# Re-laid order of the five engines within a unit of a gated delta-rule attention kernel

## The reference, cut to what matters

```python
mixed = einsum('bsh,ch->bsc', layernorm(x), W_qkv)
mixed = silu(causal_conv4(mixed, conv_w))          # q, k, v from it
q, k  = l2norm(q) * DK ** -0.5, l2norm(k)
beta, g = sigmoid(b), cumsum(-exp(A_log) * softplus(a + dt_bias))   # per chunk
A  = -(k_beta @ k.T * decay) * strict
T  = inv(eye - A)                                   # triangular, per chunk
u, kcd = T @ v_beta, T @ (k_beta * exp(g))
for chunk:                                          # the scan
    attn  = (q_i @ k_i.T) * dec_i
    v_new = u_i - kcd_i @ S
    out_i = (q_i * exp(g_i)) @ S + attn @ v_new
    S     = S * exp(g_last) + (k_i * exp(g_last - g_i)).T @ v_new
y = (rmsnorm(out) * norm_w * silu(z)) @ W_out.T
x = x + layernorm(y)
x = x + layernorm(ffn(layernorm(x)))                # weights of the ffn: lut[index]
```

## Time and profile before

| | us |
|---|---|
| median of 3 runs | 4471.09 (4470.88 to 4472.41) |
| the profiled execution, its own time | 4472.62 |
| its span, first to last instruction | 4470.8 |
| PE busy | 4252.6 (95%) |
| DVE busy | 3483.3 (78%) |
| POOL busy | 3039.3 (68%) |
| ACT busy | 2976.3 (67%) |

### The profile page before, as it was taken

The page is one execution under the profiler, slowest core; times in us unless marked ns, Lnnn a source line. Parts: engine busy times, 40 slices in busy tenths (PEclk is TensorE's granted clock), DMA queues, the critical chain, the costliest instruction groups (busy, mean ns, idle before and its releaser), DMA issues. The chain is left out here.

```text
span 4470.8 us, 92997 instructions
## 1 busy us (share of the span) xinstructions
PE 4252.6 (95%) x30644; PEld 3229.0 (72%) x30644; DVE 3483.3 (78%) x7803; ACT 2976.3 (67%) x6124; POOL 3039.3 (68%) x8989
## 2 busy tenths in 40 slices
PE   4899999999999999999999999999999999998798
PEld 2577777777777777777777777777777777777465
DVE  6678888888888888888888888888888888886554
ACT  3576777767776777667777777677767777675211
POOL 1677777777777777777777777777777777776221
PEclk7899999999999999999999999999999999999899
DMA  4222222222232222232222222232222222221200
GB/s 135 54 69 59 62 61 59 63 66 69 45 79 60 60 59 63 61 77 57 57 71 67 60 55 66 63 77 48 67 70 68 56 59 62 67 58 29 67 15 24
DMA packets 592257, 275.23 MB, mean 62 GB/s; under 512 B 464416, under 2 KB 548896, under 8 KB 582560
## 3 DMA queue, kind: packets, MB, share of 16 engines
q1 hardware_dynamic: 591056, 266.66, 24.3%
q0 software_dynamic: 720, 2.62, 0.3%
HBM read 221.87 MB, written 47.30 MB: 60 GB/s over the span
## 5 line engine op out<-in xcount | busy, mean ns | idle before, releaser
L718 DVE SCALAR_TENSOR_TENSOR CV<-pp,CW,CV 128x1023 f32<-128x1023 f32 (+2 forms) x768 | 979.5, 1275 | 30.2 <-ACT CV L1080 18.9
L343 PE MATMUL pp<-A,W 128*128 128x512 f32 x2048 | 966.8, 600 | 31.4 <-DVE CV L718 19.9
L1377 POOL TENSOR_TENSOR UL<-UL,TM 128x126 f32<-128x126 f32 (+22 forms) x1984 | 739.6, 373 | 155.4
L1374 POOL TENSOR_TENSOR TM<-UL,XL 128x126 f32<-128x126 f32 (+22 forms) x1984 | 705.4, 356 | 153.6 <-issue 19.0
L343 PEld LDWEIGHTS pp<-A,W 128*128 128x128 f32 x2048 | 376.6, 193 | 339.7 <-issue 306.8
L1176 ACT ACTIVATE QE<-qa,TAB 128x128 f32<-128x128 f32 x1024 | 316.9, 361 | 407.9 <-PE qa L472 407.8
L838 DVE SCALAR_TENSOR_TENSOR St<-St,TAB,kv 128x128 f32<-128x128 f32 x1024 | 308.5, 343 | 321.5 <-PE kv L491 313.7
L1187 ACT ACTIVATE VS<-qa,EB 128x128 f32<-128x128 f32 x1024 | 318.0, 363 | 297.1 <-PE qa L482 290.9
L535 PE MATMUL emit<-Wo,NTr 128*128 128x256 f32 x2048 | 494.7, 385 | 1.3 <-ACT NTr L1220 1.3
L514 PE MATMUL emit<-Wz,A 128*128 128x256 f32 x2048 | 491.0, 383 | 3.5 <-DVE A L889 3.5
L1080 ACT ACTIVATE CV<-pp,CW 128x1024 f32<-128x1024 f32 x256 | 284.8, 1113 | 233.3 <-PE pp L343 233.3
(11 more groups left out here) (235 smaller groups left out, 9213.9 us busy)
## 6 DMA issues: line engine op xcount, KB each, us to landing
GB<-gcd SPq DMA_DIRECT2D x64, 1024.0 KB, 5.0
W<-wqkv SPq DMA_DIRECT2D x256, 128.0 KB, 3.8
XL<-xb SPq DMA_DIRECT2D x128, 256.0 KB, 4.0
UL<-c_u SPq DMA_DIRECT2D x64, 256.0 KB, 2.9
xb<-X SPq DMA_DIRECT2D x512, 32.0 KB, 1.7
Wz<-wz SPq DMA_DIRECT2D x64, 256.0 KB, 2.8
ub<-UL SPq DMA_DIRECT2D x128, 128.0 KB, 2.9
N<-ub SPq DMA_DIRECT2D x256, 64.0 KB, 2.3
```

The lines of the kernel that those rows point to most:

```text
L343: ins = t.matmul(bk.pp[:, 512 * h:512 * h + 512], m.W[:, c, k, :], m.xnT[:, w // KH % 2, c, 512 * h:512 * h + 512], start=c == 0, stop=c == 1)
L718: v.scalar_tensor_tensor(m.CV[:, t, d:S], bk.pp[:, 0:S - d], m.CW[:, w % KH, t, 3 - d:4 - d], m.CV[:, t, d:S], ALU.mult, ALU.add).then_inc ...
L1374: gp.tensor_tensor(m.TM[:, 0:a, 0:b], m.UL[:, 0:a, k:k + 1].to_broadcast([128, a, b]), m.XL[:, k, k + 1:32].unsqueeze(1).to_broadcast([128 ...
L1377: gp.tensor_tensor(m.UL[:, 0:a, k + 1:32], m.UL[:, 0:a, k + 1:32], m.TM[:, 0:a, 0:b], ALU.subtract).then_inc(s["sub"], 1)
```

## The change

Nothing is computed in another way. The lists of the five engines for one turn of the loop are written in another order. The instruction counts are the same, except for ACT_TABLE_LOAD, which the compiler places: 379 in the program before, 131 now (four fewer in a turn). The core of the diff:

```diff
 main_sp
         for u in range(NU + 2):
+            ldt(u + 1)
             index(u + 2)
-            ldz(u + 1)
-            ldt(u + 1)
             decoded(u + 1)
+            ldw(u + 3, 1)
             ldg(u + 3)
             uo(u + 1)
-            ldw(u + 3, 1)
-            sto(u - 2)
+            ldo(u + 1)
             nl(u + 1)
+            ldw(u + 3, 2)
             ui(u + 2)
+            ldz(u + 1)
             xo(u + 2, 0)
             xo(u + 2, 1)
             xl(u + 2)
-            ldw(u + 3, 2)
             ldw(u + 3, 3)
+            ldw(u + 3, 0)
             ldx(u + 4)
-            ldo(u + 1)
-            ldw(u + 3, 0)
+            sto(u - 2)
 main_pe
             ctp(u, 0)
+            tpq(u + 2, 0)
             ks(u, 4)
             qs(u, 4)
-            tpq(u + 2, 0)
-            op(u, 0)
             tpq(u + 2, 1)
             vn(u, 4)
+            op(u, 0)
+            sup(u, 4)
             tpk(u + 2, 0)
-            sup(u, 4)
             at(u, 4)
+            ks(u, 5)
             tpk(u + 2, 1)
-            ks(u, 5)
             qs(u, 5)
-            pj(u + 2, 2, 0)
+            z(u, 1)
             kq(u + 2, 0)
             vn(u, 5)
-            z(u, 1)
+            pj(u + 2, 2, 0)
+            pj(u + 2, 2, 1)
             sup(u, 5)
             at(u, 5)
+            kq(u + 2, 1)
             ks(u, 6)
-            kq(u + 2, 1)
             qs(u, 6)
             ctp(u, 1)
-            pj(u + 2, 2, 1)
             vn(u, 6)
             op(u, 1)
             sup(u, 6)
+            at(u, 6)
             kq(u + 2, 2)
-            at(u, 6)
             z(u, 2)
-            m1(u + 1)
             ks(u, 7)
             qs(u, 7)
-            ctp(u, 2)
+            m1(u + 1)
             kq(u + 2, 3)
             vn(u, 7)
             m2(u + 1)
+            ctp(u, 2)
             sup(u, 7)
...
 main_dve
             x(u + 1, 1)
             att(u + 1, 1)
+            vt(u)
+            oacc(u - 1, 1)
             red(u - 1, 2)
-            vt(u)
+            state(u - 1, 6)
             seed(u - 1, 2)
-            oacc(u - 1, 1)
-            state(u - 1, 6)
             x(u + 1, 2)
+            core(u - 1, 6)
             att(u + 1, 2)
-            core(u - 1, 6)
+            r_(u - 1, 7)
+            cvk(u + 1, 2, 1)
+            y1r(u)
             nrm(u - 1, 2)
-            r_(u - 1, 7)
-            y1r(u)
-            cvk(u + 1, 2, 1)
             cvk(u + 1, 2, 2)
+            lm(u + 1, 1)
             cvk(u + 1, 2, 3)
+            x(u + 1, 3)
+            oacc(u - 1, 2)
             core(u - 1, 7)
-            x(u + 1, 3)
-            lm(u + 1, 1)
+            lm(u + 1, 2)
+            state(u - 1, 7)
             v10(u)
+            red(u - 1, 3)
+            seed(u - 1, 3)
+            s0(u)
             att(u + 1, 3)
-            state(u - 1, 7)
-            red(u - 1, 3)
-            s0(u)
-            oacc(u - 1, 2)
-            seed(u - 1, 3)
             cvk(u + 1, 3, 1)
...
 main_act
             nt(u - 1, 0)
-            sq(u - 1, 1)
             qsq(u + 1, 0)
             qe(u - 1, 4)
+            sq(u - 1, 1)
+            vs(u - 1, 4)
             qsq(u + 1, 1)
-            vs(u - 1, 4)
             vne(u - 1, 4)
```

More of the change, by code:

```diff
@@ L641, in loop @@
             sup(u, 1)
+            at(u, 1)
             ctp(u - 1, 3)
-            at(u, 1)
             tpv(u + 1, 1, 0)
@@ L649, in loop @@
             m4(u)
+            tpv(u + 1, 1, 1)
             sup(u, 2)
@@ L990, in loop @@
             core(u - 1, 0)
+            nrm(u - 2, 3)
             r_(u - 1, 1)
-            nrm(u - 2, 3)
             state(u - 1, 1)
             core(u - 1, 1)
+            cvk(u + 1, 0, 1)
             r_(u - 1, 2)
-            cvk(u + 1, 0, 1)
+            cvk(u + 1, 0, 2)
             red(u - 1, 0)
-            cvk(u + 1, 0, 2)
             oacc(u - 2, 3)
+            cvk(u + 1, 0, 3)
             state(u - 1, 2)
+            seed(u - 1, 0)
             core(u - 1, 2)
-            seed(u - 1, 0)
-            cvk(u + 1, 0, 3)
+            ulr(u - 1, 1)
+            lm(u + 1, 0)
             r_(u - 1, 3)
             nrm(u - 1, 0)
-            ulr(u - 1, 1)
             state(u - 1, 3)
@@ L1009, in loop @@
             cvk(u + 1, 1, 1)
+            r_(u - 1, 4)
             cvk(u + 1, 1, 2)
-            r_(u - 1, 4)
             cvk(u + 1, 1, 3)
+            state(u - 1, 4)
+            core(u - 1, 4)
+            oacc(u - 1, 0)
             red(u - 1, 1)
-            oacc(u - 1, 0)
-            state(u - 1, 4)
+            r_(u - 1, 5)
             seed(u - 1, 1)
-            core(u - 1, 4)
-            lm(u + 1, 0)
-            r_(u - 1, 5)
             kred(u + 1)
@@ L1055, in loop @@
             ulr(u, 0)
-            lm(u + 1, 2)
             cvk(u + 1, 3, 2)
@@ L1286, in loop @@
         for u in range(NU + 2):
+            vev(u, 1, 0)
             qe(u - 1, 2)
-            vev(u, 1, 0)
             vs(u - 1, 2)
             vne(u - 1, 2)
+            qt(u + 1)
+            sz(u - 1, 0)
             qe(u - 1, 3)
-            sz(u - 1, 0)
-            qt(u + 1)
             vs(u - 1, 3)
+            vev(u, 1, 1)
             vne(u - 1, 3)
             cv0(u + 1, 1)
-            vev(u, 1, 1)
             nt(u - 1, 0)
-            sq(u - 1, 1)
             qsq(u + 1, 0)
             qe(u - 1, 4)
+            sq(u - 1, 1)
+            vs(u - 1, 4)
             qsq(u + 1, 1)
-            vs(u - 1, 4)
             vne(u - 1, 4)
@@ L1309, in loop @@
             qe(u - 1, 5)
+            sz(u - 1, 1)
             dec(u + 1, 0)
@@ L1312, in loop @@
             vne(u - 1, 5)
-            sz(u - 1, 1)
+            cv0(u + 1, 2)
             dec(u + 1, 1)
+            sq(u - 1, 2)
             qe(u - 1, 6)
-            sq(u - 1, 2)
             nt(u - 1, 1)
-            cv0(u + 1, 2)
             vs(u - 1, 6)
@@ L1321, in loop @@
             dec(u + 1, 2)
+            dec(u + 1, 3)
             sz(u - 1, 2)
+            qe(u - 1, 7)
             y1l(u)
-            qe(u - 1, 7)
             vs(u - 1, 7)
@@ L1327, in loop @@
             nt(u - 1, 2)
-            dec(u + 1, 3)
-            sq(u - 1, 3)
             u12l(u)
             u12r(u)
+            sq(u - 1, 3)
             cv0(u + 1, 3)
@@ L1334, in loop @@
             qe(u, 0)
+            vs(u, 0)
+            y2(u, 1)
+            vne(u, 0)
             vev(u + 1, 0, 0)
-            vs(u, 0)
-            vne(u, 0)
-            y2(u, 1)
             sz(u - 1, 3)
@@ L1341, in loop @@
             vs(u, 1)
+            vne(u, 1)
             vev(u + 1, 0, 1)
-            vne(u, 1)
             cv0(u + 2, 0)
@@ L1517, in loop @@
             sub(u + 1, 9)
+            la(u + 1, 3)
             sub(u + 1, 10)
@@ L1521, in loop @@
             sub(u + 1, 13)
-            la(u + 1, 3)
+            ng(u + 1)
+            ixf(u + 2)
+            sub(u + 1, 14)
             tv(u, 0)
-            ng(u + 1)
-            sub(u + 1, 14)
+            sub(u + 1, 15)
+            sub(u + 1, 16)
             on(u, 0)
-            sub(u + 1, 15)
-            ixf(u + 2)
-            sub(u + 1, 16)
             sub(u + 1, 17)
@@ L1536, in loop @@
             sub(u + 1, 23)
-            tv(u, 1)
             sub(u + 1, 24)
@@ L1541, in loop @@
             sub(u + 1, 27)
+            tv(u, 1)
             sub(u + 1, 28)
@@ L1545, in loop @@
             on(u, 1)
-            vsc(u + 1, 0)
+            la(u + 2, 0)
             gm(u + 3, 0)
             gm(u + 3, 1)
+            vsc(u + 1, 0)
             tv(u, 2)
@@ L1552, in loop @@
             vsc(u + 1, 1)
-            la(u + 2, 0)
+            la(u + 2, 1)
+            la(u + 2, 2)
             tv(u, 3)
-            la(u + 2, 1)
             on(u, 3)
-            la(u + 2, 2)
     return start, loop
```

1 line of the change is left out of this document (removed).

## The result

| | before | after |
|---|---|---|
| median, us | 4471.75 (4470.88 to 4473.16, 4 runs) | 4436.78 (4436.32 to 4437.97, 4 runs) |
| span of the profiled execution | 4470.8 | 4435.0 |

The ratio is 0.9922, 95% interval 0.991 to 0.9934: 35 us or 0.78% faster, where 51 us had been forecast. The time lies 17 us above the predicted 4420 and inside its range.

The account below looks back on a forecast made before the run. PE was taken to bound the kernel, busy 95% of the span. 0.63 us a unit over some 62 units is 39 us, plus 12 irregular, 51 in all: 4472.6 to 4421.6, on the median 4420; range 4384 to 4452.

Parts of the forecast that it names:

- The bound and the waits removed: PE sets the time; its waits for St (40.2 us), strip (20.2), weight tile (6.3) and evicted bank (2.7) were costed.
- Chunk 6: `kq` ahead of `ks` 6 gains 0.93 us, `sup` 5 0.06, `z` 0.10; `vn` 6 waiting for QE costs 0.56.
- Chunk 4: Strip's wait of `tpk` gone, 0.59 us; new waits at `tpq` 1 and `vn` 4 0.53; net gain 0.06 a unit.
- Chunk 7: `m1` behind `ks` and `qs` 7, `ctp` 2 behind `m2`: `op` 2 loses cover, cost 0.14 us a unit.
- The boundary: Between units: St sooner gains 0.06 us, `ulr` starting at 3.27 instead of 3.44 gains 0.12; together 0.18.
- The unit's sum: All gains and costs in one regular unit net to 0.63 us saved; unit of 62.25 us.
- The irregular part: Late weight tiles and some `z` waits in the regular stretch, mean above ordinary unit: 12 us of 15.3 gained.
- over some 62 units: The unit's gain of 0.63 us taken over some 62 units: 39 us.
- More gain: Rival: `vn` 6 not late because ACT reaches `qe` earlier; 36 us more, 4384; chance 0.10.
- Half the gain: Rival: DVE's chain from `core` 5 to `core` 6 loses 0.5 us a unit; 31 us back, 4451; chance 0.10.
- The inverse's blocks late: Rival: Wo ahead of the loads of N makes `z` 2 1.4 us late each unit; 87 us, 4507; chance 0.05.
- A drain with each switch of table: Rival: each table switch costs ACT 1.38 us more, `vn` 6 1.0 later; 62 us, 4482; chance 0.02.

## Why the prediction was right in kind, and its time 17 us too low

**The bound and the waits removed: right.** The four waits that the change was costed for are gone from the list of waits, and PE is still what sets the time.

**Chunk 6: right in the sum, wrong in its parts.** At the place itself the 0.93 went, `sup` 5 gave its 0.06 (0.49 to 0.43), and the new cost at `vn` 6 is 0.56 from `ctp` and 0.05 ahead of it, less 0.05 at `op`: 0.56, as laid. (The laid steps add up to 2415.00 for QE, not 2415.02; it changes nothing.) The 0.10 of `z` 2 came too: it takes 1.73, where it took 1.92 with 0.09 of that for the change to `m1`'s small products. But the reason for the 0.93 was said too simply. It was put down to `kq`, which fills 0.86. With `kq` put back in the changed kernel only 0.40 return, and `kq` moved alone brings nothing in the old one. The other half comes, by the starts, from the two half projections ahead of `sup` 5, which free DVE for St. The term was right because the whole order was laid, not because the edit has that price. The cause of the new cost was half right too: the last link, `sq`, counts for little; without it `qe` waits for `qs`, and 0.08 is all that is won.

**Chunk 4: 0.06 forecast, about nothing measured.** The strip's wait gave 0.60 (0.59 laid). `tpq` 1 came 0.13 late (0.24 laid), `vn` 4 0.41 late (0.21 laid), and 0.07 were bared: 0.61 of new waits for 0.53.

**Chunk 7: right.** `op` 2 and the `at` ahead of it cost 0.16 (0.14 forecast).

**The boundary: 0.18 forecast, 0.08 measured.** St came sooner, 0.06 as forecast (the first step 1.13 to 1.07). The second term, 0.12 for `ulr`, gave 0.02 (`tpv` to `vn` 0.95 to 0.93). `ulr` does start sooner, 3.35 into the unit for 3.44, without a step of DVE ahead of it, but the blocks it copies are not there at 3.27. Of its 0.09, 0.06 are St's again, since the blocks themselves moved forward with it. The same gain was counted twice.

**The unit's sum, in part luck.** 0.63 was forecast and 0.60 measured (62.93, the mean with SP's new list alone, to 62.33). Chunk 4, chunk 7 and the boundary brought 0.19 less than laid. Some 0.16 that no term had made most of it good: 0.05 in chunks 1 to 3 (`tpv` and `sup` 2 together 0.93 for 0.97), the rest in small parts, most of them behind `vn` 6.

**The irregular part: right.** 15.3 us between mean and ordinary unit fell to about 1, and SP's list alone does 12.5 of it; no wait for W is left.

**The step that failed: "over some 62 units".** The gain of a unit was multiplied by every unit, as if first and last turn were units like the rest. They run the same lists without the work that covers them. Of the 13.3 us lost there, the runs give back 7.1 at the start and 5.8 at the end by changing places in one turn only. Without these 12.9 us the changed kernel would stand at 4423.9, within 4 us of the forecast; this is a sum of two runs' parts, and no run had both edits alone. The rows of the start lay in the old trace, and would have shown `kq` and the projection waiting there for DVE, with nothing to hide another step behind.

**The rivals.** More gain: no, `vn` 6 is as late as laid. Half the gain, by DVE's chain: no wait of `qs` for CO is in the list. The inverse's blocks late: no; `vt` waits for N once in the 61 units, for 0.2 us. A drain with each switch of table: the Trainium skill (ScalarE: Activation LUTs, "What ACT_TABLE_LOAD costs") adds about 1.38 us to each. The trace does not agree: in the run with two loads back the next step starts 1.30 behind the load's start (2416.44 to 2417.74, 2419.36 to 2420.65), and the delay of `vn` by 1.97 is explained by two times 1.30 without anything more.

## What to carry to other kernels

Where one list drives prologue, steady state and epilogue, sum them apart: the order laid for the steady state cost 13.3 us here in the first and last turn, old places put back there gave nearly all of it back, and one restored place alone only bared the next. A wait of the bounding engine brings its worth only if the engines that feed the next two or three steps are early too; `kq` moved alone brought nothing. An eviction that a later step needs belongs into the idle gap ahead of a step that waits, not behind it: that one line gave 22 us.

## What the runs showed of the hardware

Waits of PE of some 2.3 us cost more than themselves here. In the run with two loads back, PE waits 2.3 us in each unit. In 25 of the 61 units the granted clock fell behind it, and the unit took 65.6 us or more instead of 64.25; in the others it stayed, with a wait as long. What decides between the two is open. One such place (windows; the first is the wait):

```profile
2291.00:2293.00 2.00, 0.01 (x1) 0.04 (x1) 1.08 (x3) 2.00 (x7) 2.00 (x2) 1.00 0.80 246
2293.00:2297.00 4.00, 4.00 (x13) 3.43 (x14) 2.59 (x5) 3.24 (x12) 0.87 (x1) 0.57 0.33 76
```

```profile
2293.93 3.14 PE L535 MATMUL emit<-Wo,NTr 128*128 128x256 f32 x8
```

`op` takes 3.14 us in a stretch of granted clock 0.57, near the lower level, and 1.96 in the changed kernel at 1.00. Over 61 units this is 41 us (64.92 less 64.25, times 61), more than the 14 by which this run passes theory A's 4580. It is the same as at the end of the changed kernel, behind 2.36 us. With waits of 0.3 us, twice or three times a unit, the clock was 1.00 throughout.

Next, the change between the 128-wide products and the 32- and 64-wide ones costs PE about 0.1 us each way: in both kernels `qs` 0 takes 0.53 ahead of `m34` where a `qs` takes 0.43, and in the changed one `kq` takes 0.97 behind `m1` for 0.86. In no order tried here did it go away.
